# A perceiver layer on one core: local scores as four column tiles ahead of the weighing, local values with router columns behind the keys, and the second expert matrices in a ring of half buffers

## What is computed

```
x = x + xattn(layernorm(x), ctx)       # 16 heads, 32 queries against 257 keys in each batch
x = x + local_attn(layernorm(x))       # one head of 256, row s sees rows s-2 .. s+2 of its own batch
x = x + moe(layernorm(x))
# moe, for 2048 rows, 8 experts, each row goes to one:
#   logits = x @ Wr + br; expert = argmax(logits)
#   h = gelu(x @ W1[e] + b1[e])        # 256 -> 1024
#   h = gelu(h @ W2[e] + b2[e])        # 1024 -> 512
#   y = h @ W3[e] + b3[e]              # 512 -> 256
```

## Time and profile before

| | |
|---|---|
| Median of 3 runs | 742.54 us (741.34 to 744.79) |
| The profiled execution | 742.61 us, of which 740.9 us are the span of the trace |
| Busy, share of the span | PE 96%, PEld 81%, DVE 63%, ACT 61%, POOL 57% |
| First stage, tail and routing, second stage | about 0 to 417 us, 417 to 452 us, 452 to 741 us |

### The profile page before, as it was taken

How to read it: one execution, slowest core, us unless ns; L and a number is a source line. 1 busy time by engine, 2 the same in 40 slices (tenths; PEclk the granted TensorE clock), 3 DMA queues, 4 the chain that set the end, 5 groups by cost and what they waited for, 6 DMA issues and landing times.

```text
span 740.9 us, 26310 instructions
## 1 busy us (share of the span) xinstructions
PE 707.6 (96%) x9211; PEld 601.9 (81%) x9212; DVE 470.0 (63%) x1381; ACT 452.7 (61%) x1073; POOL 422.7 (57%) x562
## 2 busy tenths in 40 slices
PE   8999999999999999999999848999999999997995
PEld 7888888888888888888888737887888888886884
DVE  4466677667776777777776569969923880288000
ACT  4666666666666666676666254565665757564654
POOL 6466656565565555555654104575757776675553
PEclk9999999999999999999999988999999999998999
DMA  7222332324232333334332903256026422271000
GB/s 219 89 79 83 82 89 78 92 65 105 78 90 66 79 96 83 80 74 92 86 81 95 341 29 100 93 180 223 22 100 211 145 79 78 86 256 36 21 7 1
DMA packets 55439, 73.92 MB, mean 100 GB/s; under 512 B 6269, under 2 KB 41118, under 8 KB 55392
## 3 DMA queue, kind: packets, MB, share of 16 engines
q1 hardware_dynamic: 49248, 60.36, 27.9%
q0 software_dynamic: 2944, 8.13, 3.6%
q10 hardware_dynamic: 3200, 4.80, 1.8%
HBM read 66.90 MB, written 7.27 MB: 100 GB/s over the span
## 4 chain that ended last, share of the span: by engine, by line
PE 84%; DVE 9%; DMA 3%; ACT 1%; issue 1%; POOL 0%; SPq 0%; POOLq 0%; ACTq 0%; DVEq 0%
PE ps_s L1748 15%; PE ps_kv L1366 11%; PE ps_kv L1374 11%; PE ps_p L1413 7%; PE ps_o L1399 6%; PE ps_s L1385 5%; DVE w L1339 3%; PE ps_kv L1696 3%; PE ps_p L1696 3%; PE ps_o L1762 3%; DVE w L1336 2%; PE ps_m L1512 2%; PE ps_m L1465 2%; PE ps_m L1444 2%; PE ps_s L1728 2%; PE ps_m L1517 2%
## 5 line engine op out<-in xcount | busy, mean ns | idle before, releaser
L1007 DVE CUSTOM_DVE_ANT_0 prob<-ps_s,mask_add 128x257 f32<-128x257 f32 x256 | 94.8, 422 | 66.8 <-PE ps_s L1385 66.8
L780 ACT ACTIVATE prob<-prob,neg_max 128x257 f32<-128x257 f32 x256 | 111.2, 500 | 41.7 <-DVE neg_max L1007 40.2
L1339 DVE TENSOR_TENSOR w<-w_raw,w 128x512 fp32r<-128x512 f32 x112 | 105.3, 943 | 3.7
L1336 DVE CAST w<-w_raw 128x512 fp32r<-128x512 f32 x94 | 63.4, 674 | 69.0 <-DMA w_raw<-in_L_ffn_W_dram 69.0
L612 POOL TENSOR_TENSOR ctx_parts<-ctx_raw,ctx_parts 128x512 fp32r<-128x512 f32 x64 | 82.8, 1293 | 31.5 <-ACT ctx_parts L775 30.5
L1748 PE MATMUL ps_s<-w,h_hi 128*128 x368 | 93.7, 406 | 7.2 <-DVE w L1339 5.9
L1748 PEld LDWEIGHTS ps_s<-w,h_hi 128*128 128x128 f32 x368 | 68.5, 191 | 25.5 <-issue 10.4
L1366 PE MATMUL ps_kv<-ctx_parts,wkv_hi 128*128 128x256 f32 x512 | 85.7, 295 | 0.2 <-POOL ctx_parts L612 0.2
L1374 PE MATMUL ps_kv<-wkv_hi,ctx_parts 128*128 128x256 f32 x512 | 84.9, 293 | 1.0 <-ACT kT L784 1.0
L717 POOL TENSOR_TENSOR h_lo<-h,h_hi 128x512 fp32r<-128x512 f32 x46 | 65.0, 1413 | 25.3 <-ACT h_hi L898 20.6
L788 ACT COPY v<-ps_kv 128x512 f32<-128x512 f32 x64 | 37.5, 585 | 66.6 <-PE ps_kv L1374 66.6
(11 more groups left out here) (259 smaller groups left out, 1534.6 us busy)
## 6 DMA issues: line engine op xcount, KB each, us to landing
w_raw<-in_L_ffn_W_dram SPq DMA_DIRECT2D x24, 1024.0 KB, 7.8
ctx_raw<-in_ctx_turned_dram SPq DMA_DIRECT2D x63, 256.0 KB, 3.6
mask_add<-mask_dram SPq DMA_DIRECT2D x64, 128.5 KB, 3.4
rows_dram<-x3n ACTq DMA_DIRECT2D x16, 256.0 KB, 4.3
w_raw<-in_L_ffn_W_dram SPq DMA_DIRECT2D x8, 512.0 KB, 5.1
xt<-in_x_dram SPq DMA_DIRECT2D x16, 128.0 KB, 2.0
xr<-in_x_dram SPq DMA_DIRECT2D x16, 128.0 KB, 2.2
slot_x<-rows_dram,slot_ids POOLq DMA_INDIRECT x23, 3.7
```

The source lines that it names most:

```text
L780: a.activation(prob[:, g, :], prob[:, g, :], ACT.Exp, bias=neg_max[:, g:g + 1], scale=-1.0).then_inc(exp_done, 1)
L1007: d.tensor_tensor_reduce(prob[:, r, :], ps_s[r][:, 0:J], mask_add[:, k, :], -(HD ** -0.5), 3.0e38, ALU.add, ALU.min, neg_max[:, r:r + 1]). ...
L1336: d.tensor_copy(w[:, b, HI, part], raw[:, b, part]).then_inc(rounded, 1)
L1339: last = d.tensor_tensor(w[:, b, LO, part], raw[:, b, part], f32(w[:, b, HI, part]), ALU.subtract)
```

## The change

**Local scores.** The 128x128 product becomes eight matmuls in array tiles of 128 rows by 32 columns, two for each of the four batches, into 32 columns of `ps_m`. They stand ahead of `weigh` in k = 3, where the router's logits stood. DVE reads the 32 columns four times over through a broadcast and masks as before.

**Local values.** They move from before `keys` to behind `keys` in k = 3, and take 273 columns: 256 values, 8 columns of value times router, the key bias, and 8 columns of the row's own logits. The product of probabilities and values takes 264 columns. The router's logits then come out of sums on DVE (three instructions of 8 columns per tile in place of one), so that the transposes of the third layernorm, their copy (L1103) and `router_logits` are gone. `fuse_router` works out the 8-column weights once, in k = 1 of iteration 1: eight matmuls on PE, and on DVE three reductions and scalings, a copy and three 8-column sums. POOL gets one more instruction per tile (variance times reciprocal deviation). SP gets two more loads at the start (the turned value weights and a bias).

**Probabilities turned.** The PE transpose of the local probabilities (L1431) becomes a DVE transpose in blocks of 32x32.

**Weights.** W2 gets a ring of five half buffers, W3 two buffers of its own. The first half of W2 of expert e may now be loaded when expert e-3 is through `layer2`, the second when e-2 is. Small buffers of the first stage move into the ring's space.

```diff
-    COLS1, COLS23 = D // P * F1, F1 // P * F2 + F2 // P * D
-    BUFFERS1, BUFFERS23 = 3, 2
+    COLS1, COLS2, COLS3 = D // P * F1, F1 // P * F2 // 2, F2 // P * D
+    BUFFERS1, RING, BUFFERS3 = 3, 5, 2
...
-        LATE = [(True, 2)]
+        LATE = [(FIRST, 2), (HALVES[0], 2)]
         for e in range(2, E):
-            LATE += [(True, e + 1)] * (e + 1 < E) + [(False, e)]
+            LATE += [(FIRST, e + 1)] * (e + 1 < E) + [(HALVES[1], e), (THIRD, e)] + [(HALVES[0], e + 1)] * (e + 1 < E)
...
+            def local_scores(ps):
+                for c in range(2):
+                    for b in range(BT):
+                        last = t.matmul(ps[b * S:(b + 1) * S, :], lqk[:, c, b * S:(b + 1) * S],
+                                        turned4[:, c * P + b * S:c * P + (b + 1) * S], start=(c == 0), stop=(c == 1), skip_group_check=True)
+                return last
...
                     if k == 2:
                         middle(T, k)
-                    if k == 3 and has_local:
-                        router_logits(T)
...
+                    if k == 3 and has_out:
+                        my_turn(T, 6)
+                        local_scores(ps_m[:, 3 * P:3 * P + S]).then_inc(m_filled, 1)
                     if exists(T, k - 1) and not (isinstance(T, int) and BT * T + k > B):
                         weigh(T if k else T - 1, (k - 1) % BT)
-                    if k == 3 or k == 0:
-                        middle(T, k)
                     if ahead:
                         keys(n + 1, (k + 1) % 2)
...
-                    if k == 1:
+                    if k % 2:
                         middle(T, k)
+                    if k == 1 and isinstance(T, int) and T == 1:
+                        fuse_router()
-                    if k > 1:
+                    if k == 2:
                         end(T, k)
...
+            def add_value_bias(t, ps):
+                dve.wait_ge(spread_done, t + 1)
+                d.tensor_tensor(lv[:, :], ps[:, 0:LV], bv_rows[:, :], ALU.add)
+                return d.tensor_scalar(own_logits[:, :], ps[:, OWN_LOGITS:LW_V], spread[:, 0:1], None, ALU.mult)
+            def add_own_logits(ps, at=0):
+                return d.scalar_tensor_tensor(out=raw_logits[:, :], in0=ps[:, at + D:at + D + E], scalar=lrow_inv[:, 0:1], in1=own_logits[:, :],
+                                              op0=ALU.mult, op1=ALU.add)
+            def scale_logits(t):
+                dve.wait_ge(ln_rstd[2], t + 1)
+                return d.scalar_tensor_tensor(out=logits[:, :, bass.ds(t, 1)].rearrange("p e o -> p (e o)"), in0=raw_logits[:, :],
+                                              scalar=rstd[2][:, 0:1], in1=br_rows[:, :], op0=ALU.mult, op1=ALU.add)
...
-                dve.wait_ge(tail_filled, filled("probs"))
-                d.tensor_copy(turned0[:, 2 * P:3 * P], ps_m[:, 0:P]).then_inc(tail_taken, 1)
...
-                dve.wait_ge(ln_moments[2], TILES)
-                d.tensor_scalar(xn2[:, :], x3n[:, 0:D], moments[2][:, 0:1], None, ALU.subtract).then_inc(tail_taken, 1)
-                dve.wait_ge(tail_filled, filled("router rows"))
-                d.tensor_copy(turned4[:, 2 * P:4 * P], ps_o[:, 0:2 * P]).then_inc(tail_taken, 1)
+                dve.wait_ge(raw_logits_done, 2)
+                scale_logits(t).then_inc(tail_taken, 1)
```

More of the change, by code:

```diff
@@ L359, in over_tiles @@
                 iteration(T)
-        TURNED_BY_PE = ("probs of last but one", "output", "rows of last but one", "normalised", "values", "queries and keys",
-                        "router rows of last but one", "scores", "logits of last but one", "probs", "rows", "router rows", "logits")
-        TAKEN_BY_DVE = ("probs of last but one", "output", "rows of last but one", "normalised", "values", "queries and keys",
-                        "router rows of last but one", "scores", "logits of last but one", "probs", "rows", "centred",
-                        "router rows", "logits")
+        TURNED_BY_PE = ("output", "rows of last but one", "normalised", "values", "queries and keys",
+                        "scores", "rows")
+        TAKEN_BY_DVE = ("output", "rows of last but one", "normalised", "values", "queries and keys",
+                        "scores", "rows", "logits")
         def filled(step):
@@ L1211, in last_tile @@
                                 lq_bias[:, :].unsqueeze(2).to_broadcast([P, 2, P]), ALU.add).then_inc(tail_taken, 1)
-                dve.wait_ge(tail_filled, filled("router rows of last but one"))
-                d.tensor_copy(turned4[:, 2 * P:4 * P], ps_kv[:, 0:2 * P]).then_inc(tail_taken, 1)
                 dve.wait_ge(tail_filled, filled("scores"))
@@ L1503, in end @@
                 has_q, has_out, has_local = parts(T)
-                if not (has_out or k == 2 and has_local):
+                if not has_out:
                     return
@@ L1618, in last_tile @@
                 last.then_inc(tail_filled, 1)
-                pe.wait_ge(tail_taken, taken("probs of last but one"))
-                t.matmul(ps_kv[:, D:2 * D], turned0[:, 2 * P:3 * P], lv[:, 0:D], start=True, stop=True).then_inc(tail_filled, 1)
+                pe.wait_ge(lprob_turned, TILES - 1)
+                pe.wait_ge(v_copied, B)
+                t.matmul(ps_kv[:, P:P + D + E], turned0[:, 2 * P:3 * P], lv[:, 0:D + E], start=True, stop=True).then_inc(tail_filled, 1)
                 keep_clock(18)
@@ L1626, in last_tile @@
                 for c in range(2):
[L1627 removed]
+                    last = t.matmul(ps_s[1][:, 0:LW_V], turned4[:, c * P:(c + 1) * P], lw_v[:, c, :], start=(c == 0), stop=(c == 1))
                 last.then_inc(tail_filled, 1)
```

400 lines of the change are left out of this document (204 added, 196 removed).

## The result

The changed kernel takes 737.12 us (median of 4 runs, 736.44 to 738.36) against 742.42 us (4 runs), a ratio of 0.9929 with a 95% interval of 0.9909 to 0.9949. That is 5.3 us faster where 14.2 were forecast, and it lies outside the range of 722 to 735. The profiled execution took 736.44 us, the lowest of the four; its span is 734.7 against 740.9, so the two traces differ by 6.2 where the medians differ by 5.3.

A forecast was written before the change was run, and what follows sets the result against it. PE was taken as busy nearly everywhere, with waits on DVE. Terms -4.3 (tiles 2 to 13), -0.8 (tile 14), -1.4 (tile 15), +1.9 (iteration 1), -1.5 (tail), -8.1 (second stage) sum to -14.2: 742.61 to 728.4 us, range 722 to 735.

The forecast's parts named there:

- k=2, -0.20: Batch k=2 of tiles 2 to 15: the two transposes of the third layernorm go from PE, -0.20 us a tile.
- k=3 on PE: Batch k=3: router logits and old scores go, new scores take 0.28 us; PE could start second transposes at 5.48, not 6.12.
- k=3 on DVE: Batch k=3: later values delay DVE's copy, so second transposes start at 5.91 after a 0.43 us stall; batch 6.44 against 6.65.
- k=0, "I take nothing and keep 0.1 for the range": Next rows' normalising, after POOL's later band shift, ends within 0.1 us of the next batch's first mask; cost taken 0.
- Rival A: First stage gives nothing: DVE's chain longer or POOL's later band shift holds k=0; 0 per tile, not -0.36; 732.7 us; chance 0.20.
- k=1, +0.05: Batch k=1: 8 more columns and one 8-column sum ahead of DVE's copy cost +0.05 us, bound 0 to 0.15.
- Iteration 1, +1.9: Iteration 1: fused router weights cost 16 passes, 2.0 us, less 0.1 in k=3: +1.9 us.
- Tile 15 and tail, -2.9: Tile 15: earlier second transposes and k=2, -1.4 us; tail from last mask to last logits shorter, -1.5 us.
- Second stage, -8.1: Layer 2: earlier half loads remove the waits and slow passes, 6.65 us at slot 18 and 1.47 at slot 4.
- B: DVE's chain in k=3 is shorter, so the 0.43 us stall is not lost in iterations 1 to 13: 722.8 us; chance 0.17.
- C: Second stage: the ring does not help, a late load or splitting leaves a wait; the 8.1 goes: 736.5 us; chance 0.08.
- D: Local scores in k=3: column tiles do not overlap, 2.0 us in place of 0.28 in 15 tiles: 754.2 us; chance 0.04.

The follow-up runs named there:

- stats_ahead: Changed kernel, but in k=3 DVE takes the next rows' statistics before the value bias and POOL their power before the band shift: 726.52 us, ratio 0.9790.
- norm_ahead: stats_ahead, with DVE normalising the next rows before it masks the local scores: 723.97 us, ratio 0.9756.
- no_loop: raw_late with tiles 2 to 13 written out in place of the loop over them: 721.06 us, ratio 0.9717.
- raw_late: norm_ahead, with DVE in k=1 adding the own logits behind its copy of the transposed probabilities, not ahead of it: 722.92 us, ratio 0.9741.
- ring_as_two: Changed kernel with its memory layout, but order and waits of the weight loads as they were before: 743.86 us, ratio 1.0027.
- values_ahead: Changed kernel with the values and router columns put back ahead of the keys in k=3: 730.46 us, ratio 0.9839.

## Why the prediction was wrong

**k=2, -0.20.** Right, -0.21 to -0.22.

**k=3 on PE.** Right in place and nearly in size. The local scores took 0.24 where 0.28 was taken, inside the bounds of 0.17 and 0.32. By the rule of some 60 cycles for each matmul (the Trainium skill, TensorEngine Tiling (Array Packing), Instruction Overhead), the estimate for 16 passes is 0.40; the trace disagrees, 0.015 us a pass against 0.025. In stats_ahead, where DVE no longer holds them, the second transposes stand at 5.36; 5.48 was forecast.

**k=3 on DVE.** Right: the value bias at 3.94 (forecast 4.08), the copy at 5.10 (5.16), the second transposes at 5.85 (5.91). What was left out is that this group, which has waited, takes 0.67 to the next scores in place of 0.53: 6.52 in place of 6.44. Why was not tested.

**k=0, "I take nothing and keep 0.1 for the range".** This step failed. It compared the end of the normalising with the next batch's first mask, 1.07 us behind the scores. But DVE's mask is not the first that waits for it: PE's turning of the same rows stands at 0.62, ahead of the weighing on PE. And it gives no duration for the normalising; its "within 0.1 us" comes out with the 0.92 of the old row, where 0.52 of the split's 1.29 us was already over. Behind POOL's later power it met nearly the whole of it and took 1.35. PE stood ready at 219.94 and began at 220.56. An estimate from these rows: with 0.92 the normalising would have ended at 220.08, so some 0.2 of the 0.62 is the reader that was left out, and 0.43 the duration.

What the two cost is read against norm_ahead, where both are gone: there k=0 is 6.23. So they are 0.39 of the 0.51, 4.7 us in 12 tiles, and 0.7 in tile 14 (6.78 against 6.06), which is why the -0.8 there became -0.26. The other 0.12, 1.4 us in 12 tiles, stays in norm_ahead and is not their work: DVE's first mask stands 1.19 behind the scores there and 1.07 in the kernel before. It goes with the loop (no_loop has 0.97 and 6.00); why the loop's turn on DVE is longer in the changed kernel was not tested. Rival A named the mechanism ("POOL's later band shift holds the normalising and so k=0") but its price, 0.36 a tile at most, was too small for it: with 0.62 per tile lost it ended above even Rival A's 732.7. None of the three signs by which the forecast said it would be wrong (k=3, a wait in layer 2, long local scores) showed; what showed was "k=0 unchanged", which did not hold.

**k=1, +0.05.** Measured +0.07 in the loop, all from the place of one DVE instruction and none from the 8 columns, as raw_late shows.

**Iteration 1, +1.9.** Measured +1.70: the batch with the fused products took 8.08 against 6.32.

**Tile 15 and tail, -2.9.** Measured -2.67.

**Second stage, -8.1.** Measured -8.14, of which the ring is 6.8 by ring_as_two. The 1.47 of slot 4 went too, but not for the reason given (its first half split before W1 of expert 3): with the old order of loads it is gone as well. That part of the sum came true by luck.

**Rivals B, C, D.** B and D did not happen: DVE's chain was not shorter, and the tiles overlap. C was right to fear a late half, but none was: no layer-2 group of the changed kernel waits for DVE's weights.

## What to carry over

When an instruction is moved later on one engine, follow each consumer of every engine behind it to the first that waits, in time order: here it was not the engine that had been named but the transposes on PE half a microsecond before it. And a duration that is taken over from an old row holds only while the same instructions run beside it. And a move on PE that makes another engine late is often right in itself: the same change, with DVE's and POOL's order adapted to it (statistics in the gap while DVE waits for the values, normalising before the mask), is worth 18.5 us in norm_ahead in place of 5.3.

## What was not expected of the hardware

**DVE's normalising does not get on while POOL splits.** It is the same instruction on 128x256 from SBUF to SBUF in all these rows. Its duration is the time that it shares with POOL's split, and 0.14 or 0.15 us more:

| kernel | begins, us | split ends, us | shared | duration |
|---|---|---|---|---|
| before | 215.13 | 215.90 | 0.77 | 0.92 |
| stats_ahead | 214.07 | 215.05 | 0.98 | 1.12 |
| changed | 219.16 | 220.36 | 1.20 | 1.35 |
| values_ahead | 215.66 | 216.87 | 1.21 | 1.36 |

Begun 0.5 us ahead of the split it takes 0.48, and its fellows in k=1 and k=2 take 0.38 and 0.41. The rows of all such instructions in the changed kernel, by line (duration in ns, least, median, most):

```profile
L1031 DVE TENSOR_SCALAR xn<-xt,moments,rstd x16: 412/1348/1353, 4.8 to 372.4; 128x256 f32<-128x256 f32 x16
L1031 DVE TENSOR_SCALAR xn<-x,moments,rstd x16: 380/381/809, 52.8 to 427.5; 128x256 f32<-128x256 f32 x16
L1031 DVE TENSOR_SCALAR x3n<-x3n,moments,rstd x16: 404/410/411, 81.7 to 436.8; 128x256 f32<-128x256 f32 x16
```

The mask of the local scores, which reads its scores from PSUM, takes 0.29 beside the split in norm_ahead and 0.28 ahead of it in the changed kernel. By the Trainium skill (SBUF — State Buffer, SBUF: two separate sides), of a DVE instruction in a mode of two ports and a POOL instruction the one that starts first holds the shared pair of ports to its end, and the other fully blocks. The trace agrees: POOL began first in all four rows of the table, and DVE ended 0.14 or 0.15 behind it. Which mode DVE was in no row shows, nor why 0.15 is enough behind the split when the instruction alone takes 0.38 to 0.41.

**A loop's turn is paid by whoever is first behind it.** DVE's first mask stands 0.97 or 0.98 us behind the scores in k=1, 2 and 3 of every looped tile, and later in k=0: 1.07 in the kernel before, 1.19 in norm_ahead (1.44 in the first turn), 0.97 without the loop. The wait is put down to PE's scores, which is what hides it.
